# Second dense part of a graph and expert network: relus of a group ahead of the preceding group's normalised rows

## The reference, cut to what matters

```python
def _L1_gnn_ref(x, edge_index, edge_attr, u, batch, W1, b1, W2, b2):
    ...
    edge_attr_agg = sums / jnp.maximum(counts, 1.0)[:, None]
    combined = jnp.concatenate([x, edge_attr_agg, u_expanded], axis=1)
    h = jax.nn.relu(combined @ W1 + b1)
    return h @ W2 + b2

def _L1_ffn_ref(x, Wg, bg, W1, b1, W2, b2):
    gate_scores = jnp.einsum('bsd,ed->bse', x, Wg) + bg
    topk_scores, topk_idx = jax.lax.top_k(gate_scores, K)
    topk_probs = jax.nn.softmax(topk_scores, axis=-1)
    ...

x = x + _L1_gnn_ref(_layernorm(x, axis=-1), ...)
x = x + _L1_ffn_ref(_layernorm(x, axis=-1)[None], ...)[0]
```

## Time and profile before

| | |
|---|---|
| median of 3 runs | 3121.79 us (3117.36 to 3122.17) |
| the profiled execution | 3114.61 us, span 3112.9 us |
| TensorE matmuls busy | 2487.1 us, 80% |
| VectorE busy | 1404.1 us, 45% |
| ScalarE busy | 927.9 us, 30% |
| GpSimd busy | 1832.7 us, 59% |
| second dense part, from its first ScalarE row to its last node | 2166.4 to 2339.7 us |

### The profile page before, as it was taken

How to read it: one execution, slowest core, us unless ns; L and a number is a source line. 1 busy time by engine, 2 the same in 40 slices (tenths; PEclk the granted TensorE clock), 3 DMA queues, 4 the chain that set the end, 5 groups by cost and what they waited for, 6 DMA issues and landing times. The chain is left out here.

```text
span 3112.9 us, 48451 instructions
## 1 busy us (share of the span) xinstructions
PE 2487.1 (80%) x11766; PEld 1957.8 (63%) x11767; DVE 1404.1 (45%) x3627; ACT 927.9 (30%) x2240; POOL 1832.7 (59%) x1907
## 2 busy tenths in 40 slices
PE   2556556666667599999999892928999999999998
PEld 1344444544455466666665892928667888888898
DVE  5222225888863234333343892927784222222222
ACT  4665333333333134444433000000552111111122
POOL 6777777777777677777777777680255222322222
PEclk8787887788888789999999996969999999999999
DMA  6333334333333322222222763723586444444464
GB/s 243 104 104 104 104 104 127 105 104 104 104 104 104 94 65 62 76 65 79 73 78 74 203 188 96 214 73 107 183 255 182 107 116 107 131 103 120 111 178 136
DMA packets 216588, 372.91 MB, mean 120 GB/s; under 512 B 50437, under 2 KB 133694, under 8 KB 215231
## 3 DMA queue, kind: packets, MB, share of 16 engines
q0 software_dynamic: 82928, 157.51, 19.1%
q1 hardware_dynamic: 75772, 154.16, 15.1%
q10 hardware_dynamic: 57812, 60.35, 6.8%
HBM read 290.16 MB, written 81.71 MB: 119 GB/s over the span
## 5 line engine op out<-in xcount | busy, mean ns | idle before, releaser
L649 PE MATMUL psum<-arena 128*128 x1984 | 620.7, 478 | 361.9 <-ACT arena L401 340.1
L894 POOL DMA_INDIRECT sorted_edges<-arena x768 | 742.2, 966 | 273.8 <-issue 211.4
L341 POOL DMA_INDIRECT arena<-xn_rows,arena x784 | 747.1, 953 | 247.5 <-issue 233.5
L649 PEld LDWEIGHTS psum<-arena 128*128 128x128 f32 x1984 | 462.5, 241 | 519.7 <-issue 437.4
L401 ACT ACTIVATE arena<-arena 128x256 f32<-128x256 f32 x784 | 334.0, 496 | 576.2 <-DMA arena<-xn_rows,arena 576.2
L1179 PE MATMUL psum<-arena,acc 128*65 128x128 f32 x2720 | 312.6, 277 | 132.7 <-DVE arena L1347 132.6
L1179 PEld LDWEIGHTS psum<-arena,acc 128*65 128x65 f32 x2720 | 299.7, 139 | 145.4 <-DVE arena L1347 137.1
L1347 DVE SCALAR_TENSOR_TENSOR arena<-psum,acc 128x512 f32<-128x512 f32 x340 | 252.7, 744 | 135.9 <-DMA acc<-sorted_edges 118.8
L1765 PE MATMUL psum<-xr 128*128 128x256 f32 x1344 | 298.6, 380 | 0.9 <-DVE xr L2002 0.9
L1778 PE MATMUL psum<-arena,xr 128*128 x1344 | 297.4, 379 | 2.0 <-DVE xr L2008 2.0
L558 DVE TENSOR_TENSOR acc<-acc,psum 128x256 f32 x248 | 103.2, 416 | 430.9 <-PE psum L649 430.8
(11 more groups left out here) (318 smaller groups left out, 3145.4 us busy)
## 6 DMA issues: line engine op xcount, KB each, us to landing
xr<-in_f_W_dram SPq DMA_DIRECT2D x63, 1024.0 KB, 5.2
acc<-sorted_edges ACTq DMA_DIRECT2D x340, 132.0 KB
arena<-in_attr_dram SPq DMA_DIRECT2D x98, 264.0 KB, 2.8
arena<-xn_rows,arena POOLq DMA_INDIRECT x784, 2.7
sorted_edges<-arena POOLq DMA_INDIRECT x784
arena<-hidden_parts SPq DMA_DIRECT2D x7, 1792.0 KB, 8.3
arena<-dispatched SPq DMA_DIRECT2D x42, 265.0 KB, 2.7
arena<-in_f_W_dram SPq DMA_DIRECT2D x8, 1024.0 KB, 11.4
```

What stands on the lines that cost most here:

```text
L341: pool.indirect_dma_start(out=rows[:, c, :], out_offset=None, in_=xn_d, in_offset=bass.IndirectOffsetOnAxis(ap=idx[:, c:c + 1], axis=0)).t ...
L649: last = nc.tensor.matmul(psum[:, bank(u), 0:D], hot[:, u, c, :], rows[:, ds(slots[k] + c, 1), :].squeeze(1), start=c == 0, stop=c == RUN - 1)
L894: pool.indirect_dma_start(out=edges_d, out_offset=bass.IndirectOffsetOnAxis(ap=pos_i[:, c:c + 1], axis=0), in_=stage[:, q % PARTS, c % SC, ...
```

## The change

ScalarE's `hidden` is split in two halves of four relus. For the groups from 1 on its order was Sqrt, seven rows, eight relus, Exp; it becomes four relus, Sqrt, four relus, seven rows, Exp. VectorE keeps the aggregates of the variances (L1865) where they were; the wait for the root, the reciprocal and the product (L1867 to L1870) become `reciprocal_deviations`, which stands behind `add_parts`, the first table and `node_columns`, right before `gates`. For the last group nothing moves.

```diff
-                    def hidden(g):
-                        for q in range(8):
+                    def hidden(g, half):
+                        for q in range(half * 4, half * 4 + 4):
...
-                    hidden(0)
+                    hidden(0, 0)
+                    hidden(0, 1)
...
                     for g in range(1, NG):
+                        hidden(g, 0)
                         deviation(ln6, g - 1, s_v6, s_sd6)
+                        hidden(g, 1)
                         gate_rows(g - 1)
-                        hidden(g)
                         ratio(g - 1)
...
                         last.then_inc(s_v6, 1)
+                    def reciprocal_deviations(g):
                         dve.wait_ge(s_sd6, PHASES + g + 1)
                         own.add(nc.vector.reciprocal(ln6["rstd"][:, :], ln6["sd"][:, :]))
...
                             node_columns(g + 1)
+                        reciprocal_deviations(g - 1)
                         gates(g - 1)
...
                     deviations(NG - 1)
+                    reciprocal_deviations(NG - 1)
```

## The result

| | kernel before | changed kernel |
|---|---|---|
| median of 20 runs | 3118.84 us (3107.55 to 3128.56) | 3128.99 us (3119.60 to 3142.58) |
| ratio, with 95% interval | | 1.0034 (1.0022 to 1.0046) |
| span of the profiled execution | 3112.9 us | 3127.9 us |
| start of the second dense part's TensorE work | 2166.4 | 2171.4 |
| start of group 1's hidden products | 2205.7 | 2208.6 |

What follows compares the result with a forecast made beforehand. TensorE was taken to bound the kernel, so only its waits count. The terms 2.5 + 1.9 - 1.15 + 1.5 gave +4.8 us, 3121.79 becoming 3126.6 us, with 8 in 10 between 3119.5 and 3132.

Steps and rivals of the forecast that it cites:

- Within 0.2%: Whole kernel: the time changes by no more than 0.2%, or 6.2 us; chance 0.73.
- Relus ahead: TensorE's node 0: 0.09 us to be won in group 1, and 1.1 us earlier in group 6.
- Sums: VectorE's sums: start 0.68 us earlier but end where they did, because TensorE paces them.
- ScalarE's order: ScalarE: Sqrt's load comes among the relus, yet ScalarE is just free in time; rows run 2214.50 to 2218.05.
- Exp 1.86 us later: ScalarE's rows, load and Exp stand back to back, so VectorE's step behind the Exp comes 1.86 us later.
- +0.63 us a group: Groups 1 to 4: node sum 6 starts 0.63 us later in each, 2.5 us together.
- Group 5, +1.86: Group 5: TensorE already waits for VectorE there, so all of the lateness counts, 1.86 us.
- The rule of the Trainium skill: Table switches: about 2.66 us each by the page; the forecast used the trace's 1.30 us, seeing no such drain.
- rival C: Table switches within work cost a second 1.28 us: +18 us with the sum, 3140; chance 0.03.
- the clock: Group 5: about 3.0 us of TensorE idle time brings one slow stretch, put at 1.5 us.
- rival B: Groups 1 to 4: new TensorE holes lower the clock in each, +6 us on the sum, 3132.7; chance 0.10.
- group 6's gain of 1.15 us: Group 6: earlier node 0 ends the nodes 1.15 us sooner, and the first wide block's loads leave as much earlier.

Runs made afterwards that it cites:

- the repeat: The changed kernel run again with no edit, against the kernel before on the same chip: 3129.35 us, ratio 1.0018 (1.0003 to 1.0033).
- the other pair: Kernel before with relus ahead of the rows and spare matmuls, without and with the first experts' weights issued in group 5: 3119.20 us (0.9998) and 3112.48 us (0.9983).

## Why the prediction held, and where it did not

**The time.** 3128.99 us lies in the range of 3119.5 to 3132, 2.4 us above the forecast of 3126.6. In part that is luck: by the ratio the loss is 10.6 us (6.9 to 14.3) and not 4.8, and the forecast lands near only because it stood on 3121.79 us for the kernel before, which came out at 3118.84 in the longer series. The other runs of the changed order without spare matmuls gave less, 1.0018, 1.0024 and 1.0026, or 5.6 to 8.1 us. "Within 0.2%" had 0.73 and was wrong by the main series (1.0022 to 1.0046), though not clearly by the repeat; "slower" had 0.24.

**What held.** *Relus ahead:* node 0 of group 6 comes 6.99 us after the hidden products instead of 7.99, by 1.0 us for 1.1. *Sums:* they start 0.62 us earlier for 0.68 and end at H + 6.84 as before; TensorE paces them. *ScalarE's order:* Sqrt's load behind the fourth relu, and with nothing idle from there to the Exp. *Exp 1.86 us later:* 1.83. *+0.63 us a group:* the four periods took 2.51 us more, for 2.5. The two experiments that take one cause away each bring the period to 21.73: the Exp without its load, and VectorE's step back in its old place. *Group 5, +1.86:* with the clock held, 2.04. *The rule of the Trainium skill* on the page "ScalarE: Activation LUTs", section "What ACT_TABLE_LOAD costs", with some 1380 ns of draining behind each load: no profile here shows it; with load and Exp in the middle of work it is 1.30 us (2243.45 to 2244.75), 0.02 us behind the last row, and rival C is out.

**The term that was mis-sized: the clock.** I priced one slow stretch, behind group 5's wait for the counts, at 1.5 us. It came: nodes 4 to 6 took 7.20 us for 5.60 (and in five other profiles, 7.1 to 7.3 behind 1.5 to 2.0 us; but without the Exp they took 5.60 behind 2.01). But the clock also fell in group 5's hidden products, and that costs more than I had rows for: 10.02 for 6.25 and 2.99 for 1.72, 5.0 us together. TensorE's windows and the one idle time before it:

```profile
2298.70:2301.40 2.70, 2.70 (x6) 1.23 (x7) 2.44 (x11) 0.73 (x2) 2.09 (x3) 0.92 0.73 247
2301.40:2311.50 10.10, 10.10 (x15) 3.75 (x13) 5.52 (x18) 5.97 (x9) 7.66 (x9) 0.51 0.58 175
2311.50:2319.00 7.50, 7.45 (x33) 5.98 (x32) 5.40 (x24) 4.61 (x8) 2.21 (x3) 1.00 0.96 341
```

The granted clock is 0.51 for 10 us, 1.2 GHz, while TensorE is busy all the time, and only 0.88 us of idle time stand ahead of it (2298.67). I had taken 1.16 us as harmless from the earlier trace rows and priced only the long wait; rival B had the mechanism, idle time under a microsecond, at 0.10, but put it into groups 1 to 4 and at 1.64 us. Group 5's hidden products fell in all four profiles of the changed kernel without spare matmuls (it, its repeat, and both with earlier weights) and in the one with the Exp ahead, which has the same 0.88 us; groups 2 to 4, behind 0.81 us, fell once in twelve in the first four. In the kernel before and its version with the weights earlier, behind 0.68 to 0.8 us, none of twelve fell, but where only the relus were moved two did behind 0.68 us, groups 2 and 6, and without the Exp group 6 did behind 0.81. Counted over groups 1 to 6 of the nine profiles without spare matmuls, that is five falls in five behind 0.87 or 0.88 us and four in 49 behind 0.68 to 0.81. With the spare matmuls none of 30 fell in five profiles, behind 0.25 to 0.44 us; but only one of these five is of the changed kernel, where group 5 fell each time without them, and in group 0, which has no spare matmul ahead, the hidden products took 12.31 us in three of the five. So the idle times ahead matter, but their length alone doesn't decide. What does stays open.

**The step that failed: group 6's gain of 1.15 us.** The nodes did gain it (they end at H + 21.53, before H + 22.85, a gain of 1.3), and it went into the wait for the first wide block, 5.18 us for 3.73. I had written that SyncE issues the loads when the last node is done and that they then leave as much earlier. They do leave 1.3 us earlier (H + 22.33 for H + 23.65) but land when the DMA engines have done what is queued: 4.38 us from issue to transposes instead of 2.93. With 2 MB taken out of that stretch it is 2.92, and the wait 3.71 us again.

**The sum by its own terms**, for the profiled stretch: 2.5 for the periods; in group 5 node 0 starts 4.9 us later by the slow hidden products and reciprocals (not foreseen), the counts another 0.9 by the late Exp (1.9 forecast; the slow stretch hides the rest of it), nodes 4 to 6 take 1.6 more (1.5 forecast), less 0.1, together 7.2; 0.1 for group 6 (-1.15 forecast). The total is 9.9 us, where the forecast had 4.8.

## What to carry to other kernels

A step that is moved behind its consumer's other work moves the consumer too: ask for each result that is now later who reads it on other engines, and whether a change of table that used to hide in that reader's idle time now stands in line. Split such a change: of the two moves made here, the relus gained 0.16 us a group and the reciprocal's new place cost 0.76 (21.73 to 22.49). A gain in front of a transfer is a gain only while the DMA engines have room; read their share over the stretch ahead before counting it. And where a part in front of the edit can differ by 8 us from one execution to the next, as group 0 does here, compare the edited stretch and not the spans.

## What the runs showed of the hardware

- TensorE's granted clock fell to 1.2 GHz within hidden products that kept it busy throughout, behind 0.68 to 0.88 us of idle time, and cost about 5 us each time where reciprocals follow (9.6 to 10.1 us for 6.25, and 2.9 to 3.25 us for 1.72), 6.3 us where nodes do (9.64 and 9.75 for 6.25, then 10.31 and 10.21 for 7.38). Nodes behind 1.64 us of idle time kept 2.4 GHz behind four spare matmuls; behind a single one and 1.10 us they did not (9.10 us for 7.41).
- In the version with the Exp ahead of the rows, the table's load was done ahead of the wait where the Exp has one wait (2234.81, with the Exp at 2238.20), and behind it where the Exp has two (2281.76, Exp at 2283.06).
- From a table's load to the operation behind it it is 1.30 us, also in the middle of work (2243.45 to 2244.75, and 2236.22 to 2237.51 for the Sqrt, 1.29).
- With the DMA engines' share at 1.0, an issue by SyncE can itself be held: the first of the two weights took 9.8 us to issue (2332.20) in the changed kernel with the earlier order. That order moved the transposes by 0.16 us, less than the 0.95 us between two executions of the changed kernel; taking 2 MB out of the stretch moved them by 1.3 us and, in the other pair, by 3.15.
